# Moving the low part of the node-ordered rows from VectorE to GpSimd in a gated graph network kernel

## The chip, the core and the metric

The kernel runs on one core of one Trainium2 chip. The metric is the device time of one execution in microseconds; the time before is the median of three runs, 1602.7 us (1601.04 to 1603.7).

## What is computed

`x` is (128 batches, 128 nodes, 256 features), `adj` a 128x128 matrix. Two layers stand behind each other:

```python
x = layernorm(x + (adj @ x) @ W0 + b0)
h = x
for _ in range(3):
    a = adj @ h                                  # in_mat and out_mat are both adj
    z = sigmoid([a, a] @ w3.T + b3 + h @ u3.T + bu3)
    r = sigmoid([a, a] @ w4.T + b4 + h @ u3.T + bu3)
    c = tanh([a, a] @ w5.T + b5 + (r * h) @ u5.T + bu5)
    h = (1 - z) * h + z * c
out = layernorm(x + h)
```

## The kernel before

The 128 batches are 32 groups of 4. A group and one of its three steps is a slot; there are 96 slots, each with one graph product, five gate products, and one update of the state. Four groups are interleaved, so that slot s and slot s + 4 belong to the same group (`at(s)` gives group and step). Every matrix product is made in parts: an operand is split into a high part in a rounded type (`_hi`, written by ScalarE as a copy) and a low part, full minus high (`_lo`, an elementwise subtraction on VectorE, the helper `low_part` at L897). A product is then hi by hi, lo by hi, hi by lo: 12 matmuls of 512 columns for one gate product (L447), 6 for one graph product (L535).

A tensor of 4 batches is 128x1024. The state lies by feature (`h_t`), while the graph product needs it by node. So after an update VectorE turns 32x32 blocks (`state_blocks`, L1070) into `h_blocks`, SyncE writes them to DRAM (`write_h`), reads them back as `h_landed` (`read_h`), ScalarE copies that into `nat_hi` (`node_high`, L648) and VectorE makes `nat_lo` (`node_low`). The graph product of slot s + 2 (`graph`, L535) reads `nat_hi` and `nat_lo`; its result `ps_a` is turned in blocks (`graph_blocks`, L1015, `a_blocks`), goes through DRAM in the same way (`write_a`, `read_a`) to `a_landed`, and becomes `a_hi` and `a_lo`.

Each engine's order of work is written out by hand, as a loop over slots. In slot s:

- TensorE: `graph(s + 1)`, then the product of the state with u3, at times pieces of the first layer, then w4, w5, w3 with `a`, and last u5 with `rh` (r times h), which needs `rh_hi` and, two matmuls later in each row of six, `rh_lo`.
- VectorE: `graph_blocks(s + 1)`, the update of slot s - 1 in three operations (L1052 difference, L1055 times z, L1062 sum), `state_blocks` (once or twice), `node_low(s + 2)`, `reset(s)` (L1043 `rh`, twice, then `rh_lo`, twice), `h_lo`, `a_lo`, and work of the first layer and of the output.
- ScalarE: `node_high(s + 2)` near the start of the slot, then the copies and sigmoids of the slot.
- GpSimd: in the slots of `PRODUCT` the bias of the first layer in two halves of 128x512 (`add_bias_in_halves`, L1216), in two other slots of three small 128x4 operations of the norms (L1223 to L1235), and twice near the end a 128x1024 addition (`add_first_state`, L1256).
- SyncE: the queue of all these transfers, in one order. `read_h(m)` waits at L338 for `nat_lo` of the move two before it, because the landing buffer is used again.

In text below a slot is counted from the start of `graph(s + 1)` on TensorE. One takes 14.96, 17.86 or 16.32 us by what TensorE has to do of the first layer, in turns of three.

Of the kernel before, what the change touches and what calls it, by code (L numbers as in the profile page):

```python
# [5 lines left out]
F32 = mybir.dt.float32  # L6
F32R = mybir.dt.float32r
ALU = mybir.AluOpType
# [11 lines left out]
def gnn_kernel(nc, x, adj_t, w0, b0, w3_t, w4_t, w5_t, u3_t, u5_t, biases, out):  # L20
# [9 lines left out]
    NAT_RING = 8  # L30
# [6 lines left out]
    FOUR = 4  # L37
    ROUND = FOUR * STEPS
    SLOTS = GROUPS * STEPS
    LAST = GROUPS - 1  # L40

    def at(s):
        return FOUR * (s // ROUND) + s % FOUR, s % ROUND // FOUR
# [20 lines left out]
    def group_at(s, stage, behind=0):  # L64

        for g in LATER:
            if stage[g] + behind == s:
                return g
        return None
# [33 lines left out]
    nth_move = {step: m for m, step in enumerate(MOVES)}  # L103
# [4 lines left out]
    with ExitStack() as ctx:  # L108
        def sb(name, shape, dt=F32):
            return ctx.enter_context(nc.sbuf_tensor(name, shape, dt))  # L110

        def sem(name):
            return ctx.enter_context(nc.semaphore(name))

        def some(n, make, name, *args):
            return [make(f"{name}_{'abcdefgh'[i]}", *args) for i in range(n)]
# [19 lines left out]
        h0_nat = some(NAT_RING, sb, "h0_nat", [P, BLOCKS, C, RUN])  # L136
# [4 lines left out]
        h_landed = some(2, sb, "h_landed", [P, BLOCKS, C, RUN])  # L141
        nat_hi, nat_lo = sb("nat_hi", [P, C, COLS], F32R), sb("nat_lo", [P, C, COLS], F32R)
# [51 lines left out]
        def flat(tensor):  # L194
            return tensor[:, :, :].rearrange("p c x -> p (c x)")

        def flat_blocks(tensor):
            return tensor[:, :, :, :].rearrange("p j c x -> p (j c x)")
# [59 lines left out]
        ax_done, y_done, a_done = sem("ax_done"), sem("y_done"), sem("a_done")  # L258
        u_done, r_done, z_done, h_done = sem("u_done"), sem("r_done"), sem("z_done"), sem("h_done")

        ax_hi_ready, nat_hi_ready, h_hi_ready = sem("ax_hi_ready"), sem("nat_hi_ready"), sem("h_hi_ready")
# [4 lines left out]
        ax_lo_ready, nat_lo_ready, h_lo_ready = sem("ax_lo_ready"), sem("nat_lo_ready"), sem("h_lo_ready")  # L266
# [628 lines left out]
        def _(dve):  # L895
            def low_part(dst, full, hi):
                return dve.tensor_tensor(dst, full, hi.bitcast(F32), ALU.subtract)  # L897
# [110 lines left out]
            def graph_blocks(s):  # L1008
                n = s - FOUR
                dve.wait_ge(a_done, s + 1)  # L1010
                if n >= 1:
                    dve.wait_ge(a_written[(n - 1) % 2], ((n - 1) // 2 + 1) * 16)
                if n == 0:
                    dve.wait_ge(x_written, 2 * 16)
                tr = dve.transpose(flat_blocks(a_blocks).rearrange("p (x e) -> p x e", e=Q),  # L1015
                                   flat(ps_a).rearrange("p (x f) -> p x f", f=Q))
                tr.then_inc(a_blocks_ready, 1)

            def node_low(s):
                n, (g, t) = s - FOUR, at(s)  # L1020
                src = h0_nat[g % NAT_RING] if t == 0 else h_landed[nth_move[g, t - 1] % 2]
                dve.wait_ge(nat_hi_ready, n + 1)
                low_part(flat(nat_lo), flat_blocks(src), flat(nat_hi)).then_inc(nat_lo_ready, 1)

            def state_low(s):
                dve.wait_ge(h_hi_ready, s + 1)
                low_part(in_quadrants(h_lo), chunks_first(h_t[at(s)[0] % H_RING]),
                         in_quadrants(h_hi)).then_inc(h_lo_ready, 1)
# [20 lines left out]
            def update(s):  # L1049
                state = chunks_first(h_t[at(s)[0] % H_RING])  # L1050
                dve.wait_ge(hv_ready, 2 * s + 2)
                dve.tensor_tensor(in_quadrants(hv), in_quadrants(hv), state, ALU.subtract).then_inc(diff_ready, 1)  # L1052
                dve.wait_ge(z_ready, 2 * s + 2)
                dve.wait_ge(diff_ready, s + 1)
                dve.tensor_tensor(hv[:, :, :], hv[:, :, :], z_sb[:, :, :], ALU.mult).then_inc(scaled_ready, 1)  # L1055
                dve.wait_ge(scaled_ready, s + 1)
                if at(s) == (LAST - 1, STEPS - 1):
                    dve.wait_ge(with_first, 1)
                    dve.tensor_tensor(state, in_quadrants(hv), chunks_first(first_state[LAST - 1]),
                                      ALU.add).then_inc(h_ready, 1)  # L1060
                else:
                    dve.tensor_tensor(state, in_quadrants(hv), state, ALU.add).then_inc(h_ready, 1)  # L1062
# [84 lines left out]
            for s in range(END + 1):  # L1147
                if FOUR <= s + 1 < SLOTS:
                    graph_blocks(s + 1)
                if s == SLOTS:  # L1150
                    last_update()
                elif 1 <= s < SLOTS:
                    update(s - 1)
                    if at(s - 1)[1] < STEPS - 1:
                        state_blocks(*at(s - 1))
                for g in output_at(s, 0):
                    state_blocks(g, STEPS - 1)
                if FOUR <= s + 2 < SLOTS:
                    node_low(s + 2)
                if s < SLOTS:  # L1160
                    reset(s)
                if s == 0:
                    graph_low(1)
                    first_sum(3)
                    state_low(1)
                elif s + 1 < SLOTS:
                    state_low(s + 1)
                    graph_low(s + 1)
                if s in (0, 1):
                    first_blocks(s + 2)  # L1170
                if s == 1:
                    dve.wait_ge(adj_hi_ready, 1)
                    low_part(adj_lo[:, :], adjt[:, :], adj_hi[:, :]).then_inc(adj_ready, 1)
                if (g := group_at(s, PRODUCT)) is not None:
                    product_low(g)
                if (g := group_at(s, SUM)) is not None:
                    first_sum(g)
                if (g := group_at(s, BLOCKS_AT)) is not None:
                    first_blocks(g)
                if (g := group_at(s, TURN)) is not None:  # L1180
                    turn(g)
                if (g := group_at(s, PRODUCT, -1)) is not None:
                    turned_low(g)
                for g in output_at(s, SUM_UP):
                    residual(g)
                if s == SLOTS - 1:
                    last_prepare()
                if s == SLOTS:
                    last_statistics()
# [3 lines left out]
        def _(pool):  # L1193
# [59 lines left out]
            def add_first_state(g):  # L1253
                pool.wait_ge(h_ready, slot_of(g, STEPS - 2) + 1)
                pool.wait_ge(h0_again[g], MOVED)
                pool.tensor_tensor(first_state[g][:, :, :, :], first_state[g][:, :, :, :], h_t[g % H_RING][:, :, :, :],  # L1256
                                   ALU.add).then_inc(with_first, 1)

            def add_halves(name):
                pool.wait_ge(gate_in[name], 16)  # L1260
                w = w_raw[name]
                pool.tensor_tensor(w[:, 0:C, :], w[:, 0:C, :], w[:, C:2 * C, :], ALU.add).then_inc(gate_sum[name], 1)
# [18 lines left out]
            for s in range(END + 1):  # L1281
                for g in first_state:
                    if s == slot_of(g, STEPS - 1) - 1:
                        add_first_state(g)
                if (g := group_at(s, PRODUCT)) is not None:
                    add_bias_in_halves(g, s)
                if (g := group_at(s, MEASURE)) is not None:
                    centre(x_pass, g - FOUR, x_summed, x_centred)
                    scale_of_passes(h0_norm, x_pass, g - FOUR, x_spread_ready, x_eps_added, x_rstd_ready, x_scaled,
                                    h0_shift)  # L1290
                for g in early_output_at(s, SPREAD):
                    scale_of_passes(out_norm, out_pass, g, out_spread_ready, out_eps_added, out_rstd_ready, out_scaled,
                                    out_shift)
                for g in early_output_at(s, MEAN):
                    centre(out_pass, g, out_summed, out_centred)
                for g in output_at(s, SUM_UP):
                    if g >= LATE:
                        scale_and_shift(out_norm, g - LATE, out_var, out_var_eps, out_rstd, out_mean, out_shift,
                                        out_ready, g)
# [34 lines left out]
```

## Time and profile before

| | |
|---|---|
| median of 3 runs | 1602.7 us (1601.04 to 1603.7) |
| the profiled execution | 1605.31 us, its span 1602.9 us |
| TensorE busy | 1585.1 us, 99% |
| VectorE busy | 1395.0 us, 87% |
| ScalarE busy | 1150.6 us, 72% |
| GpSimd busy | 334.9 us, 21% |
| mean granted TensorE clock | 0.997 |

The span runs from the first to the last instruction of the program on the chip; the time of a run holds 2.4 us more. "Busy" is the union of an engine's instructions and includes the time in which an instruction that has begun waits inside for something that isn't a semaphore.

### The profile page before, as it was taken

Reading aid. Unit: us, or ns where it says so; the run is one execution under the profiler, and the core shown is the slowest. Engines: PE = TensorE matmul, PEld = TensorE weight load, DVE = VectorE, ACT = ScalarE, POOL = GpSimd, SP = SyncE. Lnnn points to the kernel's source line nnn. Section 1 sums busy time; section 2 is a strip of 40 time slices with the busy share of each in tenths; the row PEclk is TensorE's granted clock in tenths of the full one; section 3 lists DMA queues with packets and bytes.
Section 4 is the critical chain, followed back from the end, with each engine's and each line's share of the span. In section 5 each row is a group of like instructions: output and inputs, shape, how many; then the busy total and the mean of one; then the engine's idle time right before and its main releaser. Section 6 shows DMA issues by size and latency. Waiting matters only on the chain.

```text
span 1602.9 us, 21847 instructions
## 1 busy us (share of the span) xinstructions
PE 1585.1 (99%) x7404; PEld 1327.4 (83%) x7404; DVE 1395.0 (87%) x1419; ACT 1150.6 (72%) x2288; POOL 334.9 (21%) x389
## 2 busy tenths in 40 slices
PE   9999999999999999999999999999999999999996
PEld 8888888888888888888888888888788888888885
DVE  7888888889889898988989888898888898878887
ACT  4677667768777777776777677776777777776665
POOL 5111112123121231212221212212131131210013
PEclk9999999999999999999999999999999999999998
DMA  5555545775566764676646675566755566456544
GB/s 183 184 166 189 183 140 186 221 217 191 150 189 220 213 195 130 198 222 211 197 139 193 223 221 171 161 194 216 217 164 168 185 220 210 139 151 197 171 145 157
DMA packets 215759, 297.63 MB, mean 186 GB/s; under 512 B 21216, under 2 KB 184032, under 8 KB 215648
## 3 DMA queue, kind: packets, MB, share of 16 engines
q1 hardware_dynamic: 215504, 296.18, 59.4%
q8 instruction: 58, 0.95, 0.3%
q14 instruction: 53, 0.43, 0.1%
q10 hardware_dynamic: 144, 0.07, 0.0%
HBM read 149.89 MB, written 146.28 MB: 185 GB/s over the span
## 4 chain that ended last, share of the span: by engine, by line
PE 80%; DMA 7%; DVE 6%; SPq 4%; issue 2%; ACT 1%; POOL 0%; ACTq 0%; DVEq 0%
PE ps_r L447 40%; PE ps_h L447 27%; PE ps_a L535 7%; PE ps_l L492 4%; SPq L307 3%; DMA h_scratch_a<-h_blocks_a 3%; PE ps_l L502 2%; DMA h_scratch_b<-h_blocks_b 1%; DVE hv L1055 1%; DMA a_landed<-a_scratch_b 1%; DVE a_blocks L1015 1%; DMA a_landed<-a_scratch_a 1%; DMA result_b<-w_t 1%; DVE hv L1052 1%; DVE h_blocks_b L1070 1%
## 5 line engine op out<-in xcount | busy, mean ns | idle before, releaser
L1015 DVE STREAM_TRANSPOSE a_blocks<-ps_a 128x1024 f32<-128x1024 f32 x92 | 114.8, 1248 | 93.6 <-PE ps_a L535 93.4
L799 ACT ACTIVATE rh<-ps_r,bias_r 128x512 f32<-128x512 f32 x192 | 128.1, 683 | 77.8 <-PE ps_r L447 75.3
L648 ACT ACTIVATE rh_hi<-rh 128x512 fp32r<-128x512 f32 x192 | 119.0, 632 | 76.9 <-DVE rh L1043 76.7
L811 ACT ACTIVATE z_sb<-ps_r,bias_z 128x512 f32<-128x512 f32 x192 | 126.5, 681 | 37.0 <-PE ps_r L447 35.9
L1055 DVE TENSOR_TENSOR hv<-hv,z_sb 128x1024 f32<-128x1024 f32 x95 | 126.8, 1334 | 10.6 <-DVE hv L1052 0.9
L897 DVE TENSOR_TENSOR rh_lo<-rh,rh_hi 128x512 fp32r<-128x512 f32 x192 | 125.8, 689 | 9.3
L815 ACT ACTIVATE hv<-ps_h,bias_h 128x512 f32<-128x512 f32 x192 | 121.2, 677 | 12.2 <-PE ps_h L447 12.1
L447 PE MATMUL ps_r<-h_hi,u_hi 128*128 128x512 f32 x384 | 118.7, 390 | 1.6 <-ACT z_sb L811 1.5
L447 PE MATMUL ps_r<-a_hi_a,w_hi 128*128 128x512 f32 x384 | 118.8, 391 | 0.9 <-ACT rh L799 0.9
L447 PE MATMUL ps_r<-a_lo_a,w_hi 128*128 128x512 f32 x384 | 118.4, 390 | 0.5 <-DVE a_lo_a L897 0.5
L447 PE MATMUL ps_h<-rh_hi,u_hi 128*128 128x512 f32 x384 | 118.8, 390 | 0.0
L447 PE MATMUL ps_r<-a_hi_b,w_hi 128*128 128x512 f32 x384 | 118.4, 390 | 0.0
L447 PE MATMUL ps_r<-a_hi_a,w_lo 128*128 128x512 f32 x384 | 118.4, 389 | 0.0
L447 PE MATMUL ps_r<-a_hi_b,w_lo 128*128 128x512 f32 x384 | 118.3, 389 | 0.0
L447 PE MATMUL ps_r<-h_hi,u_lo 128*128 128x512 f32 x384 | 118.3, 389 | 0.0
L447 PE MATMUL ps_r<-a_lo_b,w_hi 128*128 128x512 f32 x384 | 118.3, 389 | 0.0
L447 PE MATMUL ps_r<-h_lo,u_hi 128*128 128x512 f32 x384 | 118.3, 389 | 0.0
L447 PE MATMUL ps_h<-rh_lo,u_hi 128*128 128x512 f32 x384 | 118.2, 389 | 0.0
L447 PE MATMUL ps_h<-rh_hi,u_lo 128*128 128x512 f32 x384 | 118.2, 389 | 0.0
L1223 POOL TENSOR_TENSOR x_neg_mean<-x_total,to_neg_mean 128x4 f32<-128x4 f32 x28 | 25.5, 910 | 367.4 <-ACT x_in_c L678 106.0
L447 PEld LDWEIGHTS ps_r<-h_hi,u_hi 128*128 128x128 f32 x384 | 71.7, 188 | 17.3 <-ACT z_sb L811 2.6
L447 PEld LDWEIGHTS ps_r<-a_lo_a,w_hi 128*128 128x128 f32 x384 | 72.0, 188 | 16.0 <-DVE a_lo_a L897 1.0
(381 smaller groups left out, 4295.5 us busy)
## 6 DMA issues: line engine op xcount, KB each, us to landing
h_scratch_a<-h_blocks_a SPq DMA_DIRECT2D x48, 512.0 KB, 5.0
h_landed_a<-h_scratch_a SPq DMA_DIRECT2D x192, 128.0 KB, 2.8
h_scratch_b<-h_blocks_b SPq DMA_DIRECT2D x47, 512.0 KB, 4.2
h_landed_b<-h_scratch_b SPq DMA_DIRECT2D x188, 128.0 KB, 3.0
a_scratch_a<-a_blocks SPq DMA_DIRECT2D x46, 512.0 KB, 2.7
a_landed<-a_scratch_a SPq DMA_DIRECT2D x184, 128.0 KB, 2.9
a_scratch_b<-a_blocks SPq DMA_DIRECT2D x46, 512.0 KB, 2.7
a_landed<-a_scratch_b SPq DMA_DIRECT2D x184, 128.0 KB, 3.0
```

Of the source, the lines that this page charges most:

```text
L307: sp.dma_start(landed[to * Q:(to + 1) * Q].rearrange("q i c x -> q i (c x)"), by_target[to]).then_inc(moved, 16)
L447: mm = pe.matmul(psum[:, o, :], w[:, c, o * P:(o + 1) * P], v[:, c, :], start=start and n == 0 and c == 0, stop=stop and n == 2 and c == C ...
L492: mm = pe.matmul(by_node(ps_l)[:, b, :], v[:, b * C + c, :], w[:, c, :], start=n == 0 and c == 0, stop=n == 2 and c == C - 1, skip_group_c ...
L502: mm = pe.matmul(ps_l[:, half, :], w[:, :], v[:, half, :], start=k == 0, stop=k == 2, skip_group_check=True)
L535: mm = pe.matmul(ps_a[:, c, :], w[:, :], v[:, c, :], start=k == 0, stop=k == 2, skip_group_check=True)
L648: return act.activation(dst, src, ACT.Copy)
L799: act.activation(rh[:, c, :], ps_r[:, c, :], ACT.Sigmoid, bias=bias_r[:, c:c + 1]).then_inc(r_ready, 1)
L811: act.activation(z_sb[:, c, :], ps_r[:, c, :], ACT.Sigmoid, bias=bias_z[:, c:c + 1]).then_inc(z_ready, 1)
L815: act.activation(hv[:, c, :], ps_h[:, c, :], ACT.Tanh, bias=bias_h[:, c:c + 1]).then_inc(hv_ready, 1)
L897: return dve.tensor_tensor(dst, full, hi.bitcast(F32), ALU.subtract)
L1015: tr = dve.transpose(flat_blocks(a_blocks).rearrange("p (x e) -> p x e", e=Q), flat(ps_a).rearrange("p (x f) -> p x f", f=Q))
L1055: dve.tensor_tensor(hv[:, :, :], hv[:, :, :], z_sb[:, :, :], ALU.mult).then_inc(scaled_ready, 1)
```

## The change

`node_low` is taken out of VectorE's loop and becomes an instruction of GpSimd, with the same operands and type. There it stands in slot s ahead of everything but `add_first_state`: ahead of the bias halves, and of the norm operations. It waits for `nat_hi` as before, and in words for the earlier graph product to be done (`a_done`), which `nat_hi` already implies. The semaphore `nat_lo_ready`, on which TensorE and SyncE wait, is unchanged.

```diff
-            def node_low(s):
-                n, (g, t) = s - FOUR, at(s)
-                src = h0_nat[g % NAT_RING] if t == 0 else h_landed[nth_move[g, t - 1] % 2]
-                dve.wait_ge(nat_hi_ready, n + 1)
-                low_part(flat(nat_lo), flat_blocks(src), flat(nat_hi)).then_inc(nat_lo_ready, 1)
...
                 for g in output_at(s, 0):
                     state_blocks(g, STEPS - 1)
-                if FOUR <= s + 2 < SLOTS:
-                    node_low(s + 2)
                 if s < SLOTS:
                     reset(s)
...
+            def node_low(s):
+                n, (g, t) = s - FOUR, at(s)
+                src = h0_nat[g % NAT_RING] if t == 0 else h_landed[nth_move[g, t - 1] % 2]
+                pool.wait_ge(nat_hi_ready, n + 1)
+                if n >= 1:
+                    pool.wait_ge(a_done, s)
+                pool.tensor_tensor(flat(nat_lo), flat_blocks(src), flat(nat_hi).bitcast(F32),
+                                   ALU.subtract).then_inc(nat_lo_ready, 1)
...
                     if s == slot_of(g, STEPS - 1) - 1:
                         add_first_state(g)
+                if FOUR <= s + 2 < SLOTS:
+                    node_low(s + 2)
                 if (g := group_at(s, PRODUCT)) is not None:
                     add_bias_in_halves(g, s)
```

## Rows read from the trace of the kernel before

**Rows 1.** The page: the span, and busy time of the engines.

```profile
span 1602.9 us, 21847 instructions
PE 1585.1 (99%) x7404; PEld 1327.4 (83%) x7404; DVE 1395.0 (87%) x1419; ACT 1150.6 (72%) x2288; POOL 334.9 (21%) x389
```

**Rows 2.** Stretches: length, then PE, PEld, DVE, ACT, POOL busy (instructions), clock, DMA share, GB/s.

```profile
0.00:78.00 78.00, 75.14 (x448) 66.86 (x449) 63.27 (x102) 43.39 (x68) 27.52 (x37) 1.00 0.60 188
78.00:1575.00 1497.00, 1494.65 (x6889) 1248.51 (x6889) 1310.81 (x1269) 1093.32 (x2196) 297.30 (x336) 1.00 0.60 186
1147.00:1164.00 17.00, 15.82 (x68) 12.40 (x67) 15.22 (x15) 15.04 (x30) 1.24 (x1) 1.00 0.53 182
1575.00:1603.00 28.00, 15.35 (x69) 12.02 (x68) 20.88 (x50) 13.90 (x26) 10.08 (x16) 0.81 0.40 135
```

**Rows 3.** Timeline of slot 47: start, us, engine, line, what [idle before <-releaser].

```profile
805.78 1.06 ACT L648 ACTIVATE nat_hi<-h_nat_b 128x1024 fp32r<-128x1024 f32 x1
807.02 1.22 DVE L1055 TENSOR_TENSOR hv<-hv,z_sb 128x1024 f32<-128x1024 f32 x1
...
808.28 1.22 DVE L1062 TENSOR_TENSOR h_t_g<-hv,h_t_g 128x1024 f32<-128x1024 f32 x1
...
809.42 1.22 DVE L897 TENSOR_TENSOR nat_lo<-h_nat_b,nat_hi 128x1024 fp32r<-128x1024 f32 x1
...
810.56 1.29 DVE L1043 TENSOR_TENSOR rh<-rh,h_t_h 128x512 f32<-128x512 f32 x2
...
815.24 0.62 PE L447 MATMUL ps_h<-rh_hi,u_hi 128*128 128x512 f32 x2
```

**Rows 4.** One tile's instructions (ns min/median/max), and a group by line (busy, mean ns).

```profile
L897 DVE TENSOR_TENSOR nat_lo<-h_landed_a,nat_hi x39: 1180/1183/2564, 69.0 to 1537.9; 128x1024 fp32r<-128x1024 f32 x39
L1256 POOL TENSOR_TENSOR h_t_b<-h_t_b,h_t_h 128x1024 f32<-128x1024 f32 x1 | 2.4, 2410 | 0.0
```

**Rows 5.** Timelines of slots 51 and 54, GpSimd beside VectorE.

```profile
869.82 2.36 POOL L1216 TENSOR_TENSOR x_in_b<-x_in_b,bias_row 128x512 f32<-128x512 f32 x1
...
869.84 1.18 DVE L1052 TENSOR_TENSOR hv<-hv,h_t_c 128x1024 f32<-128x1024 f32 x1
...
921.66 1.29 POOL L1216 TENSOR_TENSOR x_in_c<-x_in_c,bias_row 128x512 f32<-128x512 f32 x1
924.11 1.30 POOL L1216 TENSOR_TENSOR x_in_c<-x_in_c,bias_row 128x512 f32<-128x512 f32 x1 [1.16 <-DVE h_t_b L1062]
...
921.68 2.36 DVE L1062 TENSOR_TENSOR h_t_b<-hv,h_t_b 128x1024 f32<-128x1024 f32 x1
924.07 1.25 DVE L1070 STREAM_TRANSPOSE h_blocks_a<-h_t_b 128x1024 f32<-128x1024 f32 x1
```

**Rows 6.** Timeline of slot 87, which begins at 1455.4.

```profile
1459.25 1.07 ACT L648 ACTIVATE nat_hi<-h_landed_b 128x1024 fp32r<-128x1024 f32 x1 [2.99 <-DMA h_landed_b<-h_scratch_b]
...
1460.65 1.22 DVE L1062 TENSOR_TENSOR h_t_g<-hv,h_t_g 128x1024 f32<-128x1024 f32 x1
...
1465.31 1.28 DVE L1043 TENSOR_TENSOR rh<-rh,h_t_h 128x512 f32<-128x512 f32 x2
...
1467.61 0.62 PE L447 MATMUL ps_h<-rh_hi,u_hi 128*128 128x512 f32 x2
```

**Rows 7.** Timeline of slot 66, with bias halves on GpSimd.

```profile
1118.76 2.35 DVE L1062 TENSOR_TENSOR h_t_f<-hv,h_t_f 128x1024 f32<-128x1024 f32 x1
...
1124.55 1.28 DVE L1043 TENSOR_TENSOR rh<-rh,h_t_g 128x512 f32<-128x512 f32 x2
1125.93 1.30 DVE L897 TENSOR_TENSOR rh_lo<-rh,rh_hi 128x512 fp32r<-128x512 f32 x2
...
1120.80 1.04 ACT L648 ACTIVATE nat_hi<-h_landed_b 128x1024 fp32r<-128x1024 f32 x1
...
1128.85 0.62 PE L447 MATMUL ps_h<-rh_lo,u_hi 128*128 128x512 f32 x2
```

**Rows 8.** Timeline of slots 67 and 68: the longest gap of TensorE, and ScalarE before it.

```profile
1149.69 0.50 PE L447 MATMUL ps_r<-h_hi,u_hi 128*128 128x512 f32 x1 [1.18 <-ACT z_sb L811]
...
1147.42 1.06 ACT L648 ACTIVATE a_hi_a<-a_landed 128x1024 fp32r<-128x1024 f32 x1 [5.91 <-DMA a_landed<-a_scratch_a]
```

**Rows 9.** The waits of SyncE's queue: who waited for whom, us in total, times, longest.

```profile
SPq L338 <- DVE nat_lo L897: 2.9, 2, 2.1
```

## Prediction, made before the changed kernel was built or run

> **What bounds the kernel.** I read the page's busy shares first. TensorE is busy for 1585.1 of 1602.9 us [rows 1], and VectorE, which the change relieves, for 1395.0: it is second, not first. So the next question is where TensorE's missing 17.8 us lie, and the table of stretches answers it [rows 2]: 2.86 us before 78 us, 2.35 us in the 1497 us from there to 1575, and 12.65 us in the last 28. The moved operation runs 92 times, the first at 69 us, the last two slots ahead of the end. It can reach neither the start nor the tail, where other work of the norms and the last update stands. What is left for it to win is 2.35 us, half of it in one gap of 1.18 us in slot 68 [rows 2, 8]. In the rest of the slots VectorE's work is hidden behind matmuls that follow each other without a gap, and its time matters only where it is late for one of them. The granted clock is 1.00 in all stretches up to 1575 [rows 2], so nothing is to be had from the clock either.
>
> **How much room VectorE has.** In the ordinary slot 47, `rh` is finished at 811.85 (810.56 + 1.29), and TensorE first reads what is made from it at 815.24 [rows 3]: 3.4 us of room. Slot 87 has 1.02 us (1465.31 + 1.28 = 1466.59 against 1467.61) [rows 6]. Room of this kind, slot by slot, decides the case, not VectorE's busy share.
>
> **The change, part by part.**
>
> 1. *What leaves VectorE.* 92 subtractions of 1.18 us (median) [rows 4], 109 us. One that starts at 809.42 lets the next begin at 810.56 [rows 3], so its place in the queue is 1.14 us.
>
> 2. *What comes to GpSimd.* The same form, two 128x1024 f32 tensors of SBUF into one, took 2.41 us there [rows 4]. 92 of them are 222 us; GpSimd then has some 557 us of 1603, and is not the bound. The type of the result (fp32r) is not seen on GpSimd in this trace; by the row it costs the same, and the end of 2.41 us is kept for both bounds, with up to 0.2 us more as the far end.
>
> 3. *What the two engines do to each other.* This is the term that decides. In slot 54 a bias half on GpSimd runs from 921.66 to 922.95, and VectorE's L1062, issued at 921.68, takes 2.36 us in place of 1.22: it stood until GpSimd was done and then ran [rows 5, 3]. In slot 51 it is the other way: L1052 takes its ordinary 1.18 us, and the bias half issued in the same moment takes 2.36 us in place of 1.29 [rows 5]. The transpose at 924.07 runs at 1.25 us right across a bias half [rows 5]. So a GpSimd operation and a VectorE operation with two SBUF inputs exclude each other, in the order in which they come, and transposes are free. Hence a moved `node_low` doesn't take 1.14 us from VectorE; it takes 1.14 us away and puts up to 2.41 us in front of the next two-input operation, unless that time falls on transposes or on a semaphore wait.
>
>    The Trainium skill has this as a rule ("SBUF — State Buffer", section "SBUF: two separate sides": the shared port pair is an exclusive lock for a whole instruction, and a VectorE operation with two SBUF inputs takes it against GpSimd). The same page adds, under "A bandwidth-pool intuition that's wrong", some 115 ns from the end of the one to the start of the other. The rows don't show that: 869.84 + 1.18 + 1.29 is 872.31, and the bias half had ended at 872.18. By the page's figure each of the thin slots below would come out about 0.1 us worse, an estimate, and the sum some 1 us higher.
>
> 4. *Where it falls.* It depends on when `nat_hi` is finished. **Early**: in slot 47 that is 806.84, before L1055 begins; GpSimd holds the ports to about 809.3, L1055 waits from 807.02 to there, and everything behind it comes 2.3 us later, less the 1.14 us of the operation that is gone: `rh` about 1.15 us later, with 3.4 us of room [rows 3]. Nothing is lost. **In the middle**: in slot 87 `nat_hi` is finished at 1460.32, within L1055; GpSimd goes ahead of L1062 and keeps it from 1460.65 to about 1463.0; `rh` comes 1.2 us later against 1.02 us of room: TensorE stands 0.2 us [rows 6]. I found three slots near the end with so little room and take 0.3 us for each: +0.9 us. **Late**: where `nat_hi` is finished while L1062 runs, GpSimd gets the ports after it, half its time lies under the transposes of `h_blocks`, and `rh` comes when it came before.
>
> 5. *The bias halves.* In every third slot GpSimd has them, and `node_low` is now in front of them; they wait with it for `nat_hi`. In slot 66 this frees L1062, which had waited for the first half (2.35 us, now 1.22) [rows 7]: the `h_blocks` transposes and SyncE's write behind them come 1.1 us earlier. But the halves then fall between the operations of `rh`. `nat_hi` is finished at 1121.84, GpSimd is done at about 1124.3, `rh` begins there (1124.55 before), and 2 x 1.3 us of bias come between, so `rh_lo` is finished at about 1129.6 in place of 1127.2, against 1128.85 + 0.23 at which TensorE wants its second half [rows 7, 5]: 0.5 us of stall. About six of the slots have `nat_hi` so late, at 0.4 us each: +2.4 us.
>
> 6. *The loop through DRAM.* `h_blocks`, SyncE's queue, `a_landed`, `a_hi`, `a_lo` and back to VectorE make a loop over three slots that is nearly as long as TensorE's 49.1 us. The gap in slot 68 comes from it: ScalarE had stood 5.91 us for `a_landed` [rows 8]. With step 5 the loop gets 1.1 us back in each turn. Of the 2.35 us of gaps I take 1.3 us as closed.
>
> 7. *Waits past which it moves.* SyncE's reads wait for `nat_lo` (2.9 us in all [rows 9]); it is now finished about 2.4 us behind `nat_hi` or L1062, no later than before in most slots, so nothing changes there. TensorE needs `nat_lo` a slot later; in slot 47 it was ready at 810.64 and the slot ends at 818.0. Behind the wait for `nat_hi` GpSimd now queues bias halves (wanted a slot later) and norm operations (wanted at the end of the slot): covered, and worth under 1 us if not.
>
> **The sum**: +0.9 + 2.4 - 1.3 = +2.0 us. The profiled execution took 1605.3 us (its span and 2.4 us around it), so 1607.3 by it; it was 2.6 us above the median of 1602.7, and I give 1604.7 against the median.
>
> **Rivals.**
>
> - *A: VectorE becomes late as a rule.* If in the two slots of a turn in which VectorE is full the operation falls ahead of L1062, `h_blocks` comes 1.2 us later in each, 2.4 us in a turn, and the loop of step 6 passes TensorE's 49.1 us. For it: in slot 66 VectorE's room behind `rh_lo` is under 2 us, and most `nat_hi` of the ordinary slots come before L1062. Against: in just the full slots `nat_hi` comes late (slot 66: 1121.84 when L1062 had begun at 1118.76 [rows 7]). Four stretches with two tight turns each, less some 2 us of room in each: 4 x (4.8 - 2) = 11 us, 1614. It decides from the point at which `nat_hi` of those slots is finished before L1062 begins.
> - *B: the loop gains and nothing else is late.* The bias halves don't get in between the `rh` operations or fit into room that is there; all gaps from 78 to 1575 close: 1602.7 - 2.35 = 1600.4. For it: step 6. Against: steps 4 and 5 price stalls from rows.
> - *C: it does nothing measurable.* VectorE's saving is eaten by its own waiting for the ports, all of it inside the room: 1602.7. For it: the 3.4 us of the ordinary slot.
>
> More than 3.2 us of gain has no source after rows 2.
>
> **Chances.** Forecast (1603.5 to 1607) 0.47, A 0.22, B 0.15, C 0.16. 0.2% is 3.2 us, about what a measurement of this kernel can tell from no change. Slower by more than that (over 1605.9) is A and a third of the forecast, 0.37; faster is a corner of B, 0.03; within, 0.60. The range has to take in B's end and the lower half of A: 1600.3 to 1611.5.
>
> **What the profile after would show.** `nat_lo` on GpSimd at 2.4 us where it is alone and up to 3.6 us where it waits for a VectorE operation; VectorE's busy time not 109 us lower but near or above the old one, about 1395 - 109 + some 150 of waiting, 1440 (step 3); L1055 or L1062 at 2.3 us and more in the slots with an early `nat_hi` (step 4); L1062 back at 1.22 us in slot 66, and the bias halves beside `rh` and `rh_lo` there (step 5); the gap of slot 68 smaller (step 6), new gaps of 0.2 to 0.6 us in front of `ps_h<-rh_hi` or `rh_lo` (steps 4 and 5). TensorE's busy time stays. It would be wrong if GpSimd takes much over 2.41 us for this type, if a waiting GpSimd operation is passed over by VectorE, or if late `a_landed` become frequent (A).

## The result

The changed kernel takes 1607.8 us (median of 8 runs, 1605.57 to 1608.55) against 1602.92 us for the kernel before in the same measurement (8 runs): a ratio of 1.0028, 95% interval 1.0019 to 1.0036. It is slower, by 3 to 6 us. A second measurement, beside other kernels (`again`), gave 1.0020 (1.0011 to 1.0029).

The page of the changed kernel, the lines that answer to [rows 1], and its costliest group of matmuls that wait:

```profile
span 1606.8 us, 21938 instructions
PE 1587.6 (99%) x7404; PEld 1326.1 (83%) x7404; DVE 1438.0 (89%) x1327; ACT 1144.7 (71%) x2288; POOL 600.2 (37%) x481
...
L447 PE MATMUL ps_h<-rh_hi,u_hi 128*128 128x512 f32 x384 | 122.1, 395 | 1.7 <-ACT rh_hi L648 1.2
```

VectorE has 92 instructions fewer and is busy for 43 us longer. TensorE does the same matmuls and shows 2.5 us more of busy time and 1.4 us more of idle time. In the kernel before, the group `ps_h<-rh_hi` was busy for 118.8 us with no idle time ahead of it; the new cost is there, in front of the product that needs `rh_hi`.

The tile `nat_lo` by its instructions (ns min/median/max), for [rows 4]:

```profile
L1257 POOL TENSOR_TENSOR nat_lo<-h_landed_a,nat_hi x39: 2378/2797/3419, 65.1 to 1538.3; 128x1024 fp32r<-128x1024 f32 x39
L1257 POOL TENSOR_TENSOR nat_lo<-h_landed_b,nat_hi x25: 2395/2408/3476, 82.0 to 1552.1; 128x1024 fp32r<-128x1024 f32 x25
```

The stretch that answers to the second row of [rows 2] (length, then PE, PEld, DVE, ACT, POOL busy):

```profile
79.00:1579.00 1500.00, 1497.59 (x6889) 1247.75 (x6888) 1353.99 (x1179) 1087.60 (x2196) 558.93 (x427) 1.00 0.60 186
```

By its idle time TensorE lost nothing here: 2.41 us now, 2.35 before. That reading misleads, and it misled the prediction. A matmul of this kernel stands in the record for 0.39 us, but the next begins 0.23 us after it (two take 0.62 us). So the start of one can be 0.16 us late before any idle time shows, and one that comes late is recorded as longer, up to 0.5 us. The kernel before has such a pair in slot 68, with no idle time ahead of it:

```profile
1160.77 0.90 PE L447 MATMUL ps_h<-rh_hi,u_hi 128*128 128x512 f32 x2
```

So I measure slots by the distance from the first matmul of one graph product (L535) to that of the next, in both traces. A slot without any wait takes 14.96, 16.32 or 17.86 us. By that measure the kernel before lost 4.3 us in slots 3 to 92, not 2.35: 0.97 in slot 20, 0.49 in 44, 1.86 in 68, 0.99 in 86. The difference between the two traces, slot by slot:

| | us |
|---|---|
| closed: slots 20, 44, 68 | -0.97, -0.49, -1.33 |
| new, slots with bias halves: 9, 15, 27, 39, 45, 51, 63, 75 | +0.12 to +0.28 each, 1.74 |
| new, slots with bias halves whose ScalarE is latest: 54, 69 | +0.74 each |
| new, slot 53 | +0.97 |
| new, near the end: 87, 90, 92 | +0.56, +0.57, +0.40 |
| slots 3 to 92 together | +3.0 |
| ahead of slot 3 | +1.2 |
| behind slot 92 | -0.4 |

The 1.2 us at the start lie ahead of the change: the first graph product began 1.5 us later (22.58 us against 21.04), long before the first moved operation at 65.1 us. In `again` the start gave 0.05 us, with +2.5 us in the slots, and over all kernels below it moved between -0.2 and +1.2. I take it for chance and not for the change's.

The slots of the kernel before come from the one execution of it that was profiled. That one took 1605.31 us, 2.4 us more than the median of 1602.92, so its slots were probably longer than in most executions. The section on the experiments comes back to this.

### The profile page after: what moved, and what is told of

It reads as the page before. It is cut to its first block, busy times and chain, and to the rows that moved or that the text cites. A ratio compares the mean times of both kernels' runs of the same rounds, so it can differ in the third digit from the quotient of the medians.

```text
span 1606.8 us, 21938 instructions
## 1 busy us (share of the span) xinstructions
PE 1587.6 (99%) x7404; PEld 1326.1 (83%) x7404; DVE 1438.0 (89%) x1327; ACT 1144.7 (71%) x2288; POOL 600.2 (37%) x481
## 4 chain that ended last, share of the span: by engine, by line
PE 78%; DVE 9%; DMA 5%; ACT 3%; SPq 2%; issue 2%; POOL 1%; ACTq 0%; DVEq 0%; POOLq 0%
PE ps_r L447 38%; PE ps_h L447 27%; PE ps_a L535 7%; PE ps_l L492 4%; SPq L307 2%; PE ps_l L502 2%; DMA h_scratch_a<-h_blocks_a 2%; DVE a_blocks L1015 1%; DVE rh L1037 1%; DVE hv L1049 1%; DMA h_scratch_b<-h_blocks_b 1%; DVE hv L1046 1%; DVE h_blocks_b L1064 1%; DMA a_landed<-a_scratch_b 1%; ACT rh_hi L648 1%
## 5 line engine op out<-in xcount | busy, mean ns | idle before, releaser
L1257 POOL TENSOR_TENSOR nat_lo<-h_landed_a,nat_hi 128x1024 fp32r<-128x1024 f32 x39 | 109.4, 2805 | 332.0 <-ACT nat_hi L648 332.0
L1049 DVE TENSOR_TENSOR hv<-hv,z_sb 128x1024 f32<-128x1024 f32 x95 | 152.0, 1600 | 9.9
L811 ACT ACTIVATE z_sb<-ps_r,bias_z 128x512 f32<-128x512 f32 x192 | 123.0, 677 | 15.5 <-PE ps_r L447 14.2
L447 PE MATMUL ps_h<-rh_hi,u_hi 128*128 128x512 f32 x384 | 122.1, 395 | 1.7 <-ACT rh_hi L648 1.2
L1257 POOL TENSOR_TENSOR nat_lo<-h_landed_b,nat_hi 128x1024 fp32r<-128x1024 f32 x25 | 67.3, 2691 | 106.0 <-ACT nat_hi L648 106.0
L1221 POOL TENSOR_TENSOR h_var_eps_sb<-x_spread,eps 128x4 f32<-128x4 f32 x28 | 23.0, 823 | 185.6 <-ACT h_nat_e L684 27.6
```

The lines of the kernel that those rows point to most:

```text
L447: mm = pe.matmul(psum[:, o, :], w[:, c, o * P:(o + 1) * P], v[:, c, :], start=start and n == 0 and c == 0, stop=stop and n == 2 and c == C ...
L811: act.activation(z_sb[:, c, :], ps_r[:, c, :], ACT.Sigmoid, bias=bias_z[:, c:c + 1]).then_inc(z_ready, 1)
L1257: pool.tensor_tensor(flat(nat_lo), flat_blocks(src), flat(nat_hi).bitcast(F32), ALU.subtract).then_inc(nat_lo_ready, 1)
```

## How the new gaps come about

Slot 50 shows the ordinary case. Timelines of the changed kernel, GpSimd and VectorE:

```profile
858.13 2.41 POOL L1257 TENSOR_TENSOR nat_lo<-h_landed_a,nat_hi 128x1024 fp32r<-128x1024 f32 x1 [10.92 <-ACT nat_hi L648]
...
858.24 3.38 DVE L1056 TENSOR_TENSOR h_t_b<-hv,h_t_b 128x1024 f32<-128x1024 f32 x1
861.65 1.25 DVE L1064 STREAM_TRANSPOSE h_blocks_b<-h_t_b 128x1024 f32<-128x1024 f32 x1
862.82 1.25 DVE L1037 TENSOR_TENSOR rh<-rh,h_t_c 128x512 f32<-128x512 f32 x2
```

(L1046, L1049, L1056 and L1037 are L1052, L1055, L1062 and L1043 of before.) GpSimd had the ports at 858.13, L1056 came 0.11 us later and took 3.38 us in place of 1.22: 2.2 us of waiting for 1.14 us of work removed. `rh` is 1.1 us later in its slot than before, within its room. In slot 87 the room was smaller [rows 6]; the same again, now with TensorE:

```profile
1463.12 2.47 POOL L1257 TENSOR_TENSOR nat_lo<-h_landed_b,nat_hi 128x1024 fp32r<-128x1024 f32 x1 [9.76 <-ACT nat_hi L648]
...
1463.35 3.31 DVE L1056 TENSOR_TENSOR h_t_g<-hv,h_t_g 128x1024 f32<-128x1024 f32 x1
...
1468.99 1.25 DVE L1037 TENSOR_TENSOR rh<-rh,h_t_h 128x512 f32<-128x512 f32 x2
...
1470.37 1.10 PE L447 MATMUL ps_h<-rh_hi,u_hi 128*128 128x512 f32 x2
```

Two matmuls take 1.10 us where two take 0.62 without a wait, and no idle time is shown before them: this is the loss that a busy share hides.

Slot 51 has the bias halves. GpSimd, ScalarE, VectorE and TensorE of the changed kernel:

```profile
868.88 1.18 POOL L1221 TENSOR_TENSOR h_var_eps_sb<-x_spread,eps 128x4 f32<-128x4 f32 x1 [7.20 <-ACT h_nat_e L684]
870.14 1.01 POOL L1223 TENSOR_TENSOR h_rstd_sb<-h_var_eps_sb,minus_half 128x4 f32<-128x4 f32 x1
871.23 1.10 POOL L1225 TENSOR_TENSOR h_mean_rstd<-x_neg_mean,h_rstd_sb 128x4 f32<-128x4 f32 x1
872.41 1.25 POOL L1227 TENSOR_TENSOR h_shift<-h_mean_rstd,sixteen 128x4 f32<-128x4 f32 x1
876.80 2.40 POOL L1257 TENSOR_TENSOR nat_lo<-h_landed_b,nat_hi 128x1024 fp32r<-128x1024 f32 x1 [3.14 <-ACT nat_hi L648]
879.17 2.99 POOL L1208 TENSOR_TENSOR x_in_b<-x_in_b,bias_row 128x512 f32<-128x512 f32 x2
...
873.69 2.08 ACT L721 ACTIVATE h_nat_e<-x_in_a,h_shift,h_rstd_sb 128x256 f32<-128x256 f32 x4 [3.74 <-POOL h_shift L1227]
875.68 1.05 ACT L648 ACTIVATE nat_hi<-h_landed_b 128x1024 fp32r<-128x1024 f32 x1
...
882.74 0.63 ACT L648 ACTIVATE rh_hi<-rh 128x512 fp32r<-128x512 f32 x1 [1.07 <-DVE rh L1037]
...
879.18 3.53 DVE L1037 TENSOR_TENSOR rh<-rh,h_t_d 128x512 f32<-128x512 f32 x2 [1.91 <-ACT rh L799]
...
883.06 0.87 PE L447 MATMUL ps_h<-rh_hi,u_hi 128*128 128x512 f32 x2
```

The two engines take turns: bias half, `rh`, bias half, `rh`. Each `rh` waits for the half that came just ahead of it, and the pair takes 3.53 us in place of 1.28. The second `rh_hi` comes late and TensorE stands 0.27 us. But there is more in these lines than the prediction had: the slot's `nat_hi` is finished 8.8 us after its start, before it was 5.8. The cause is the small norm operations. In the kernel before, the last two of them were done in a moment (below them its `nat_hi`):

```profile
869.39 0.20 POOL L1233 TENSOR_TENSOR h_mean_rstd<-x_neg_mean,h_rstd_sb 128x4 f32<-128x4 f32 x1
869.67 0.20 POOL L1235 TENSOR_TENSOR h_shift<-h_mean_rstd,sixteen 128x4 f32<-128x4 f32 x1
...
871.88 1.05 ACT L648 ACTIVATE nat_hi<-h_landed_b 128x1024 fp32r<-128x1024 f32 x1
```

The small operations came just ahead of VectorE's update. By the two traces, in the changed kernel VectorE's `rh` was 1.1 us late in the slot before, and ScalarE's squares (L684), for which the first small operation waits, were 0.75 us late. The four small operations begin late enough to meet the update, and now each of the last two waits for one whole VectorE operation: 1.10 and 1.25 us. `h_shift`, and with it ScalarE's norm (L721), `nat_hi` and the sigmoid for `rh`, come up to 3 us later. 0.75 us of delay has become 3.

How late the second `rh` may end is seen from the slots with bias halves. In slots 21, 30 and 66 the halves took the same turns with `rh`, the second `rh` ended 14.3 to 14.4 us into the slot, and nothing was lost. In slot 51 it ended at 14.8 (0.27 us lost), in slot 54 at 15.25 (0.74 lost). Slot 66 is the one from which the prediction had worked out 0.5 us.

## The experiments

Ratios are to runs of the kernel before on the same chip; "slots" is the change of slots 3 to 92 in the profiled execution against the kernel before.

| kernel | ratio (95% interval) | slots, us |
|---|---|---|
| the change, first time | 1.0028 (1.0019 to 1.0036) | +3.0 |
| again | 1.0020 (1.0011 to 1.0029) | +2.5 |
| nobody | 0.9990 (0.9981 to 0.9999) | -3.2 |
| bias_first | 1.0030 (1.0019 to 1.0041) | +2.7 |
| after_update | 1.0001 (0.9992 to 1.0009) | -1.7 |
| no_bias | 1.0007 (0.9998 to 1.0016) | -0.8 |
| port_only | 1.0080 (1.0058 to 1.0103) | +14.9 |
| halves | 0.9994 (0.9984 to 1.0003) | -3.2 |
| tuned | 0.9991 (0.9982 to 1.0000) | -2.9 |
| tuned_again | 0.9996 (0.9987 to 1.0005) | -2.8 |
| halves_tuned | 0.9999 (0.9991 to 1.0008) | -2.6 |

The medians and the slots differ, always in the same direction: in ten of the eleven rows the kernel's median lies 1.4 to 2.6 us further above that of the kernel before than the column of slots says (for the change +4.9 us by medians, for `nobody` -1.4). Only `port_only`, with four runs, has both at 15 us. That fits a profiled execution of the kernel before that was some 2 us slower than usual. So differences between two changed kernels in this column are safer than the difference of one to the kernel before. A second trace of the kernel before, which would settle it, was not taken.

**again**, the changed kernel as it is.

> The changed kernel as it is, to have its time beside the other kernels on one chip. Theory P (ports): GpSimd's subtraction keeps VectorE's two-input operations waiting, TensorE's new gaps stand in front of ps_h<-rh_hi in the slots with bias halves (some 3.2 us in all) and near the end (some 1.5 us), and 2.8 us of old gaps are closed: 1.002 to 1.0035 of the kernel before. Theory S (start): 1.2 us of the 3.9 us by which the span grew lie ahead of slot 3, where no instruction of the change runs; if that is chance in how the first loads land, it should be gone here or come in the kernel before as well.

1.0020, at the lower end of what was expected. New gaps stand in the same slots but 39, and in two more of the bias slots (+0.5 in 21, 51 and 53, +0.77 in 54, 0.2 in 33, 0.39 to 0.59 in 87, 90 and 92), and the start is as before. Both theories hold: the slots carry the cost, the start was chance.

**nobody** makes `nat_lo`, but for 4 of its 1024 columns; what VectorE's relief is worth alone.

```diff
-                pool.tensor_tensor(flat(nat_lo), flat_blocks(src), flat(nat_hi).bitcast(F32),
+                pool.tensor_tensor(nat_lo[:, 0, 0:4], flat_blocks(src)[:, 0:4], nat_hi[:, 0, 0:4].bitcast(F32),
                                    ALU.subtract).then_inc(nat_lo_ready, 1)
```

> The changed kernel, but GpSimd subtracts only 4 of the 1024 columns; the rest of nat_lo is left out, so neither VectorE nor GpSimd does that work, and waits and order stay. Theory P: without the 2.4 us on the ports the new gaps in front of rh_hi go, and the relief of VectorE is worth at most the 2.35 us of gaps of before: 0.9985 to 1.000, 1600.5 to 1603. Theory O (order): if the cost comes from the bias halves standing behind the wait for nat_hi, it stays: 1.001 to 1.003.

0.9990. Every new gap is gone and slots 20, 44 and 68 are closed in full; its group of waiting matmuls is clean:

```profile
L447 PE MATMUL ps_h<-rh_hi,u_hi 128*128 128x512 f32 x384 | 118.2, 389 | 0.0
```

So the order on GpSimd costs nothing by itself (theory O falls), and the most that taking this work off VectorE could bring is some 3.2 us in the slots and 1.4 us, 0.1%, by the medians. The difference to the changed kernel, 5.7 to 6.2 us in the slots, is the price of the ports.

**port_only**: the other side, the ports without the relief. The kernel before, with one more subtraction on GpSimd:

```diff
...
+            def stand_in(s):
+                pool.wait_ge(nat_hi_ready, s - FOUR + 1)
+                constant = gate_hi["u5"][:, :, :].rearrange("p c o -> p (c o)")[:, 0:448].unsqueeze(1).to_broadcast(
+                    [P, 2, 448]).bitcast(F32)
+                if s > FOUR:
+                    pool.wait_ge(stand_in_done, s - FOUR)
+                pool.tensor_tensor(spare[:, :, :], constant, constant, ALU.subtract).then_inc(stand_in_done, 1)
...
+                if FOUR <= s + 2 < SLOTS:
+                    stand_in(s + 2)
```

> The kernel before, VectorE keeps node_low; GpSimd gets in addition a subtraction of 128x896 at the same place in its order (two SBUF inputs, a constant, into a spare tile). It is the price of the ports alone, without VectorE's relief of 1.14 us. Theory P: rh comes some 2.2 us later in most slots, against 2.15 us of room in the ordinary short slot and 1 to 2 in the tight ones; with the loop through DRAM longer as well: 1.005 to 1.012. If the engines don't exclude each other, 1.000.

1.0080 from four runs (1611.81 to 1620.41 us), with 26 slots longer by 0.1 us or more. An operation for whose result no other engine waits, at 2.1 us each, costs 13 us in all by the ratio, 15 by medians and slots. That is more than the 5.7 to 6.2 us above, because VectorE keeps its own `node_low` here and the room of many more slots is used up. The group by line of GpSimd:

```profile
L1267 POOL TENSOR_TENSOR spare<-u_hi 128x896 bf16<-128x896 f32 x92 | 193.3, 2102 | 601.1 <-ACT nat_hi L650 601.1
```

And the same matmuls as above, on this kernel's page; against the kernel before, 5.7 us more of busy time and 8.2 us of idle time stand there:

```profile
L449 PE MATMUL ps_h<-rh_hi,u_hi 128*128 128x512 f32 x384 | 124.5, 398 | 8.2 <-ACT rh_hi L650 7.2
```

**bias_first**: `node_low` behind the bias halves.

```diff
+                if (g := group_at(s, PRODUCT)) is not None:
+                    add_bias_in_halves(g, s)
                 if FOUR <= s + 2 < SLOTS:
                     node_low(s + 2)
-                if (g := group_at(s, PRODUCT)) is not None:
-                    add_bias_in_halves(g, s)
```

> The changed kernel with node_low behind the bias halves in GpSimd's slot, not ahead of them. Theory B (the bias halves between the two rh operations make the 3.2 us of gaps in those slots): those gaps go, L1056 waits for the first half again, and the gaps of slots 20, 44 and 68 come back: 1.0005 to 1.002. Theory P without B: GpSimd's subtraction itself keeps rh late there: as the changed kernel or more, 1.003.

A miss in the size, 1.0030. All ten gaps of the bias slots are gone, as theory B said; but the loop through DRAM came back for more than I had given it. Slot 53 now loses 1.69 us, slot 20 loses 1.15 where the changed kernel had closed it, 56 and 65 lose 0.2 and 0.4. The copy `a_hi_b` that slot 53 needs, in this kernel and in the changed one:

```profile
901.03 1.06 ACT L648 ACTIVATE a_hi_b<-a_landed 128x1024 fp32r<-128x1024 f32 x1 [4.64 <-DMA a_landed<-a_scratch_b]
...
900.95 1.06 ACT L648 ACTIVATE a_hi_b<-a_landed 128x1024 fp32r<-128x1024 f32 x1 [2.27 <-DMA a_landed<-a_scratch_b]
```

Slot 53 begins at 901.76 here and at 902.37 there, so `a_hi_b` comes 0.7 us later in it, which is all of the difference between 1.69 and 0.97. What one order wins the other gives back. It also shows that step 6 of the prediction, that later bias halves let `h_blocks` go earlier and shorten the loop, is real.

**no_bias**: the halves shrunk to 4 of 256 columns in the changed kernel; the rest of the bias is left out.

```diff
-                    add = pool.tensor_tensor(rows[:, b, :], rows[:, b, :],
-                                             bias_row[:, :].unsqueeze(1).to_broadcast([P, G // 2, D]), ALU.add)
+                    add = pool.tensor_tensor(rows[:, b, 0:4], rows[:, b, 0:4],
+                                             bias_row[:, 0:4].unsqueeze(1).to_broadcast([P, G // 2, 4]), ALU.add)
```

> The changed kernel, where the bias halves add 4 of 256 columns only; the rest of the first layer's bias is left out in the groups from 4 on. Theory B (the two halves between the rh operations make the gaps of slots 9, 15, 27, 39, 45, 51, 63, 75): these gaps and those of 54 and 69 go, the ones at the end (1.5 us) stay: 0.9990 to 1.0005. Rival N (ScalarE is late there, since GpSimd's four small norm operations now wait for VectorE's operations one by one, and nat_hi and the sigmoids behind it come 3 us later): the gaps stay at more than half: 1.001 to 1.002.

All ten gaps are gone; 53 (1.03 us), 87, 90 and 92 (1.5 us) stay. ScalarE is as late in slot 51 as in the changed kernel, and still nothing is lost there. ScalarE, GpSimd and VectorE of this kernel:

```profile
872.43 2.08 ACT L721 ACTIVATE h_nat_e<-x_in_a,h_shift,h_rstd_sb 128x256 f32<-128x256 f32 x4 [3.73 <-POOL h_shift L1227]
...
877.90 0.80 POOL L1208 TENSOR_TENSOR x_in_b<-x_in_b,bias_row 128x8 f32<-128x8 f32 x2
...
877.92 1.33 DVE L1037 TENSOR_TENSOR rh<-rh,h_t_d 128x512 f32<-128x512 f32 x2 [1.92 <-ACT rh L799]
```

So the late norm chain (rival N) uses up room but makes no gap alone. The bias halves among the `rh` operations do, together with it: in slots 21, 30 and 66 of the changed kernel, where ScalarE was 0.4 us less late than in slot 51, they make none either.

**after_update**: GpSimd also waits for the slot's update, so that it starts under the transposes.

```diff
                 pool.wait_ge(nat_hi_ready, n + 1)
+                pool.wait_ge(h_ready, s - 2)
```

> The changed kernel, where GpSimd's subtraction waits for h_ready of the slot as well, so that it begins when L1056 ends and runs under the transposes. Theory P: rh comes as before in all slots, the gaps near the end (1.5 us) go, ScalarE is no longer late, and VectorE's gain is left: 0.999 to 1.000, 1601 to 1603. If the place within the slot doesn't matter, 1.002 to 1.0035 as for the changed kernel.

1.0001: about 4 us of the cost by medians, 4 to 5 in the slots, go with one wait. Slots 20, 44, 68 closed, 87 and 90 clean; 0.53 us are left in slot 39, 0.33 in 54, and 0.77 in 92, where one of the two large additions of the end follows `node_low` directly and the `rh` pair takes 4.68 us.

**halves**: two instructions of 128x512 in place of one (`split_in_two` gives columns 0 to 511 and 512 to 1023).

```diff
-                pool.tensor_tensor(flat(nat_lo), flat_blocks(src), flat(nat_hi).bitcast(F32),
-                                   ALU.subtract).then_inc(nat_lo_ready, 1)
+                for half, (into, full, high) in enumerate(zip(*(split_in_two(t) for t in (
+                        flat(nat_lo), flat_blocks(src), flat(nat_hi).bitcast(F32))))):
+                    low = pool.tensor_tensor(into, full, high, ALU.subtract)
+                low.then_inc(nat_lo_ready, 1)
```

> The changed kernel with GpSimd's subtraction as two instructions of 128x512. Theory P with a lock for a whole instruction, in order of coming: VectorE gets in between the halves, L1056 or L1049 waits for 1.3 us and not 2.4, but the second half then stands in front of the next one: VectorE's operations show 1.2 us of waiting twice as often, rh comes as late as in the changed kernel less up to 0.2 us: 1.001 to 1.003. If what counts were how long GpSimd holds the ports at a time, the time would fall to 1.000.

A miss: 0.9994, not 1.001 to 1.003, and -3.2 us in the slots, as good as without the work. GpSimd and VectorE in slot 50 of this kernel:

```profile
856.21 3.54 POOL L1262 TENSOR_TENSOR nat_lo<-h_landed_a,nat_hi 128x512 fp32r<-128x512 f32 x2 [10.54 <-ACT nat_hi L648]
...
856.24 2.35 DVE L1056 TENSOR_TENSOR h_t_b<-hv,h_t_b 128x1024 f32<-128x1024 f32 x1
858.62 1.25 DVE L1064 STREAM_TRANSPOSE h_blocks_b<-h_t_b 128x1024 f32<-128x1024 f32 x1
859.79 1.25 DVE L1037 TENSOR_TENSOR rh<-rh,h_t_c 128x512 f32<-128x512 f32 x2
```

L1056 waits for the first half only, 2.35 us in place of 3.38. The second half gets the ports when L1056 is done and runs under the transpose, which doesn't need them; `rh` follows at once. My expectation had the second half in front of "the next operation" and left out that the next one is a transpose: it held the rule of step 3 and not the row beside it.

**tuned**: `after_update`, with the bias halves and the two additions of the end behind `h_lo_ready`, so that they run when both `rh` and both `rh_lo` of the slot are done.

```diff
                 pool.wait_ge(x_blocks_ready, g - FOUR + 1)
+                pool.wait_ge(h_lo_ready, s + 2)
...
                 pool.wait_ge(h0_again[g], MOVED)
+                pool.wait_ge(h_lo_ready, slot_of(g, STEPS - 1))
```

> after_update, with the bias halves and the two 128x1024 additions of the end also moved: they wait for h_lo_ready, so that they run behind the rh operations of their slot. Theory P (each thing on GpSimd costs where it stands ahead of a two-input operation for which TensorE is waiting, and nothing elsewhere): the gaps that after_update still has in slots 39, 54 and 92 (1.6 us) go, and what is left is the relief alone, as in the kernel in which nobody makes nat_lo: 0.9985 to 0.9995, about 1601. If the halves are late for the first layer there, new gaps come in slots with the first layer's products: over 1.000.

> tuned a second time, to narrow its interval: 0.9982 to 0.9998. The start, ahead of slot 3, moved by -0.2 to +1.2 us between runs of kernels that are the same there; the slots should show -2.9 us again.

0.9991 and, the second time, 0.9996, both with intervals that reach 1. The gaps of 39, 54 and 92 are gone and one of 0.4 us in slot 5 is new. The slots show -2.9 and -2.8 us, close to the -3.2 of `nobody`.

**halves_tuned**: both.

> halves (no wait for h_ready), with the bias halves and the two additions of the end behind h_lo_ready as in tuned. Theory P: both halves and tuned already have nearly no gap of the change's own, and the relief of VectorE can't close more than the gaps of slots 20, 44 and 68; so 0.9985 to 0.9998, the same as those two, about 1602. Anything under 0.998 would mean that there was more to win than the gaps in front of TensorE.

0.9999. Nothing is added; each of the two had hardly a gap of the change's left to close, and this kernel has the one in slot 5 that `tuned` has (0.42 us) and 0.17 us in slot 8. Against the changed kernel the four versions with the work placed otherwise are clearly faster (0.9991 to 1.0001 against 1.0020 and 1.0028). Against the kernel before, `tuned` and `halves` are faster by 0.6 to 1.5 us by the medians, and each of their intervals reaches 1: no gain is shown.

## Why the prediction was right, and where not

It said slower by 2.0 us, 1604.7, in a range of 1600.3 to 1611.5; measured were 1607.8 against 1602.9. The direction, the mechanism and most of the slots were right, the sum was too small: 2.0 us against 4.9 by the medians, and 3.0 in the slots. The time lies above the band of 1603.5 to 1607 that had the chance of 0.47 and below rival A's 1614. It is inside the range because that reached halfway up to A, which came true in one slot only. That part is luck.

- *What bounds it* (held, with a wrong number). Only 2.35 us to win, I said, from TensorE's idle time. The slots of that trace had lost 4.3 us, since much of a late matmul's wait shows as busy time; `nobody` gained 3.2 of it. The way to see it stood in the trace of the kernel before: pairs of matmuls longer than 0.62 us.
- *Steps 1 to 3, ports* (held). The 115 ns that step 3 quotes from the Trainium skill ("SBUF — State Buffer", section "A bandwidth-pool intuition that's wrong") are stated there for a DMA whose descriptors GpSimd writes, not for two elementwise operations, and the rows show none. VectorE's busy time was forecast at 1440 us, measured 1438.0; GpSimd's subtraction at 2.4 alone and up to 3.6 waiting, measured 2.38 to 3.48. `port_only` put the price of the ports without the relief at +0.8%, `nobody` the relief without the ports at -0.1%.
- *Step 4, thin slots near the end* (held, mis-sized). 0.9 us forecast, 1.53 measured in slots 87, 90 and 92. Slot 87 was given 0.2 us and lost 0.56: the room of 1.02 us was counted from the second `rh` to the first matmul that reads `rh_hi`. ScalarE's copy of 0.63 us lies between, and the second half is wanted 0.23 us later: the real room was 0.6 us. `rh` ended 0.95 us later in its slot, so 0.35 to 0.4 us of the 0.56 are explained by this sum; where the rest comes from isn't shown.
- *Step 5, bias halves* (right cause, mis-sized and one instruction off). 2.4 us forecast for some six slots, 3.2 measured in ten. I had the halves in front of `rh_lo`; in slot 51 one ran ahead of the first `rh` and one between the two, and it is `rh_hi` that was late. Slot 66, from which the 0.5 us had been worked out, lost nothing, as did 21 and 30; the gaps stood in other slots, where ScalarE was later. `bias_first` and `no_bias` both removed all ten gaps. That the norm chain would make ScalarE up to 3 us late and use up room was not in the sum.
- *Step 6, the loop* (direction held, size open). -1.3 forecast, -2.8 measured in slots 20, 44 and 68; `bias_first` gave part of it back in 20 and 68. But `port_only`, where VectorE keeps all its work, also has slot 44 closed and slot 68 shorter by 1.07 us. Either the later bias halves are enough for that, or the one trace of the kernel before had more than its usual gaps there.
- *Step 7* (held where tested). `nobody` keeps the waits and the order, and has no gap.
- *Rival A* came true in one place. In slot 53, where VectorE is full, `node_low` stood ahead of L1056, and 0.97 us were lost; the loop was late there too, `a_hi_b` by 0.8 us. It stayed one slot out of the eight or so that 1614 would have taken.
- The terms as measured: +1.5 + 3.2 + 1.0 - 2.8, with 0.1 in slot 86, are +3.0 us in the slots. The runs say 3 to 6 us in the first measurement and 2 to 5 in the second. The rest, some 2 us, is about what the profiled execution of the kernel before took over its median, as the section on the experiments has it; that this is the whole of it isn't shown.

## What to carry to other kernels

In this kernel, work with two SBUF inputs that was moved from VectorE to GpSimd was not simply taken off VectorE. It was exchanged for a wait of twice the length, unless it was placed under operations that don't need the shared ports, such as the transposes. One semaphore wait, or two instructions in place of one, turned +0.2 to 0.3% into nothing, and a place behind the last urgent VectorE operation closed the gaps that the bias additions still made. Where TensorE is the bound, measure slots from one fixed matmul to the next, and count the room of a step to the engine that reads it first.

## What the runs showed of the hardware

- GpSimd's f32 subtraction into fp32r costs what the addition with an f32 result does: 2.38 us at least for 128x1024, against 2.41 us for the addition in [rows 4].
- A GpSimd operation of 128x4 took 0.20 us when VectorE was not in a two-input operation and 1.10 to 1.25 us when it was, so in slot 51 a chain of small ones advanced by one step for each VectorE operation. A delay of 0.75 us of its start became 3 us at its end. The Trainium skill ("SBUF — State Buffer", section "SBUF: two separate sides") gives the rule, a lock held for a whole instruction; the trace agrees for both directions and both sizes.
- An operation that waits for the ports is recorded as running from its issue (L1056 at 3.38 us), and part of a matmul's wait for its operand is hidden as well (1.10 us for two in place of 0.62). The busy time of both engines rose while the work fell or stayed the same.
- The two engines were served in the order in which their operations came: in slot 51 bias half, `rh`, bias half, `rh` took turns, and in `halves` L1056, issued 0.03 us behind GpSimd's first half, ran ahead of the second.
- A 32x32 block transpose was not held up: in `halves` it took 1.25 us right beside GpSimd's second half.
